# A transformer layer in float16 halves on one core: the second norm and the quantiser folded into factors, the low halves of the probabilities moved to VectorE

## The reference

```python
xn = layernorm(x, eps=1e-5)
x = x + attention(xn) + ffn(xn)

def attention(x):               # 16 heads of 16
    q = x @ Wq.T; latent = x @ Wkv_down.T           # latent has 64 columns
    k, v = latent @ Wk_up.T, latent @ Wv_up.T
    att = softmax(mask(q @ k.T / 4))  # 64 keys back, and the first 4
    return (att @ v) @ Wo.T

def bitlinear(x, w):
    xn = layer_norm(x, eps=1e-6)
    g = max(abs(xn)); x_hat = clip(xn * 128 / g, -128 + 1e-6, 128 - 1e-6) * g / 128
    w_hat = sign(round(w / (mean(abs(w)) + 1e-6))) * mean(abs(w))
    return x_hat @ w_hat.T

def ffn(x):                     # hidden width 1024
    return bitlinear(gelu(bitlinear(x, w_fc)), w_proj)
```

## Time and profile before

| what | us |
|---|---|
| median of three executions | 197.97 |
| span of the profiled execution, first to last instruction | 195.3 |
| prologue, to the first `fc` tile of batch 1 | 43.98 |
| batches 1, 2, 3, each from its first `fc` tile to the next one's | 43.02, 41.93, 35.07 |
| batch 4, from its first `fc` tile to the end of the span | 31.30 |

### The profile page before, as it was taken

The page is one execution under the profiler, slowest core; times in us unless marked ns, Lnnn a source line. Parts: engine busy times, 40 slices in busy tenths (PEclk is TensorE's granted clock), DMA queues, the critical chain, the costliest instruction groups (busy, mean ns, idle before and its releaser), DMA issues.

```text
span 195.3 us, 4915 instructions
## 1 busy us (share of the span) xinstructions
PE 160.2 (82%) x1954; PEld 106.9 (55%) x1954; DVE 148.7 (76%) x261; ACT 104.3 (53%) x152; POOL 81.9 (42%) x106
## 2 busy tenths in 40 slices
PE   1827947789978499999969499999799999997953
PEld 1515512445865466556756456647667764676731
DVE  0689999996999976655999976678997877696341
ACT  2557601356999222076997122368994314899020
POOL 6240192003089800450199601430598215059830
PEclk9999955579999755899999756999999999999975
DMA  6995000001000000013000000030000002100001
GB/s 170 334 330 168 3 2 0 3 18 38 3 3 2 0 3 0 3 54 109 0 0 0 0 0 0 0 106 5 0 0 7 0 3 65 43 3 3 0 3 54
DMA packets 7836, 7.49 MB, mean 38 GB/s; under 512 B 2500, under 2 KB 7464, under 8 KB 7720
## 3 DMA queue, kind: packets, MB, share of 16 engines
q1 hardware_dynamic: 6108, 6.02, 10.2%
q10 hardware_dynamic: 1712, 1.25, 2.1%
HBM read 6.21 MB, written 1.05 MB: 37 GB/s over the span
## 4 chain that ended last, share of the span: by engine, by line
PE 51%; DVE 26%; ACT 10%; issue 8%; DMA 2%; POOL 1%; DVEq 0%; ACTq 0%; SPq 0%
PE ring L1003 7%; PE acc L1161 7%; PE ring L1028 5%; PE ring L1122 4%; PE aux L1239 3%; PE ring L1033 3%; DVE xn L734 3%; ACT E L473 3%; PE ring L1150 3%; DVE t2s L810 3%; PE ring L1216 3%; DVE gh L803 2%; ACT EH L474 2%; PE aux L1178 2%; DVE sth L785 2%
## 5 line engine op out<-in xcount | busy, mean ns | idle before, releaser
L351 POOL TENSOR_TENSOR EL<-E,EH 128x1024 f16<-128x1024 f32 x16 | 36.3, 2296 | 37.4 <-ACT EH L474 28.4
L713 DVE TENSOR_REDUCE mx<-ring 128x4 f32<-128x768 f32 x16 | 14.7, 951 | 6.3 <-PE ring L1033 6.3
L474 ACT ACTIVATE EH<-ring,un 128x1024 f16<-128x1024 f32 x16 | 17.8, 1115 | 0.0
L473 ACT ACTIVATE E<-ring,un 128x1024 f32<-128x1024 f32 x16 | 17.8, 1112 | 0.0
L1028 PE MATMUL ring<-mask,idb 128*128 128x384 bf16 (+1 forms) x48 | 14.7, 393 | 2.2 <-DVE vs L890 2.2
L1150 PE MATMUL ring<-idf,t2s 128*128 128x128 f32 x64 | 10.4, 316 | 5.8 <-DVE Q L851 5.2
L399 POOL TENSOR_SCALAR ve<-mv 128x2 f32<-128x2 f32 x4 | 1.0, 239 | 32.5 <-DVE gx L757 32.4
L487 ACT ACTIVATE gl<-ring,a 128x1024 f32<-128x1024 f32 x8 | 8.9, 1116 | 9.1 <-PE ring L1003 9.1
L1161 PE MATMUL acc<-prT,t2h 128*128 128x256 f16 x48 | 13.2, 311 | 0.0
L1122 PE MATMUL ring<-xhT,wqT 128*128 128x256 f16 x64 | 11.1, 302 | 2.5 <-ACT EH L474 2.5
L1161 PE MATMUL acc<-prT,t2l 128*128 128x256 f16 x48 | 13.1, 309 | 0.0
(11 more groups left out here) (220 smaller groups left out, 464.7 us busy)
## 6 DMA issues: line engine op xcount, KB each, us to landing
wfc_r<-in_L_ffn_w_fc SPq DMA_DIRECT2D x1, 1024.0 KB, 7.3
wpr_r<-in_L_ffn_w_proj SPq DMA_DIRECT2D x1, 1024.0 KB, 9.6
xres<-in_L_attn_x SPq DMA_DIRECT2D x4, 256.0 KB, 2.8
out<-ob SPq DMA_DIRECT2D x4, 256.0 KB, 2.2
bias<-in_c_bias SPq DMA_DIRECT2D x1, 825.0 KB
xin<-in_L_attn_x ACTq DMA_DIRECT2D x3, 256.0 KB, 2.6
wq_r<-in_L_attn_Wq ACTq DMA_DIRECT2D x1, 256.0 KB, 3.3
xin<-in_L_attn_x SPq DMA_DIRECT2D x1, 256.0 KB, 3.9
```

The source lines that it names most:

```text
L351: nc.gpsimd.tensor_tensor(EL[at].rearrange("p g t q -> p g (t q)"), E32[:, r], EH[at].rearrange("p g t q -> p g (t q)"), ALU.subtract).the ...
L473: nc.scalar.activation(E32[:, r], src[:], ACT.Exp, scale=un[:, 0:1]).then_inc(ex[0], 1)
L474: nc.scalar.activation(EH[at].rearrange("p g t q -> p g (t q)"), src[:], ACT.Exp, scale=un[:, 0:1]).then_inc(exh[0], 1)
L713: nc.vector.tensor_reduce(out=o, in_=src[:, :, 0:2 * (T - BLK)].rearrange("p a (t k) -> p a t k", t=2), axis=AX.X, op=ALU.max).then_inc(re ...
```

## The change

- The second norm of the input rows is a factor. Since `xn` has mean zero, the feed-forward part reads `xhT` and `xlT`, and the factor `rs2`, worked out on GpSimd from the variance (`vr`, `vn`, `ve2`), goes into gelu's scale `a1`. `st2`, `mv2`, `cx`, `gx`, `txs`, their four transposes and the halves `thT`, `tlT` are gone.
- The quantiser is left out as an identity, so that `ch`, the maximum `gh`, `ghr` and `t2s` are gone. TensorE transposes `gl` itself. `gh` now names the high half of the hidden rows and `glo` the low one, both scaled by 1/gamma.
- Centring the hidden rows is done in the weights: the rows of the ternary `w_proj` get their mean subtracted once (`tsum`, `tmean`, `second_ternary`).
- The low halves of the probabilities are taken on VectorE, between other steps of the batch.
- The order is written anew: no loop, one order for all four batches. The hidden rows are transposed, and their high halves made, ahead of the exponentials; the second product stands between the rounds of scores; two rounds of the maxima come before `y` is transposed; VectorE divides after it has made `VL` and `vs`.

```diff
--- before
+++ after
 # GpSimd
-            def low_half(b, r):
...
+            def row_factors(n):
...
+                nc.gpsimd.tensor_tensor(vr[:], mv1[:, :, 1], rs1[:], ALU.mult).then_inc(row2[0], 1)
...
+                nc.gpsimd.tensor_tensor(vn[:], vr[:], rs1[:], ALU.mult).then_inc(row2[0], 1)
...
+                nc.gpsimd.tensor_scalar(ve2[:], vn[:], FFN_EPS, None, ALU.add).then_inc(row2[0], 1)
...
+                nc.gpsimd.tensor_tensor(rs2[:, n % 2, :], ve2[:], neghalf[:, 0:TT_], ALU.pow).then_inc(row2[0], 1)
 # ScalarE
+            def hidden_high(b, i):
+
+                wait(act, tr_h, b, i + 1)
...
+                nc.scalar.activation(gh[:, i].rearrange("p k n -> p (k n)"), flat(slot("t2T", b, i)),
+                                     ACT.Copy, scale=gam_r[:, 0:1]).then_inc(gh_ok[0], 1)
 # VectorE
+            def second_ternary():
+
+                dve.wait_ge(w_neg, 1)
+                for c in range(CC):
+                    did_pro(nc.vector.scalar_tensor_tensor(out=neg_t[:, 0, c * F:(c + 1) * F], in0=wpr_r[:, c, :], scalar=pthr[:, 1:2],
+                                                           in1=neg_t[:, 1, c * F:(c + 1) * F], op0=ALU.is_gt, op1=ALU.subtract,
+                                                           accum_out=tsum[:, c:c + 1]))
+                settle_pro()
+                did_pro(nc.vector.tensor_scalar(tmean[:], tsum[:], 1.0 / F, None, ALU.mult))
+                settle_pro()
+                for c in range(CC):
+                    nc.vector.tensor_scalar(tern[:, 1, c * F:(c + 1) * F], neg_t[:, 0, c * F:(c + 1) * F], tmean[:, c:c + 1], None,
+                                            ALU.subtract).then_inc(w_tern, 1)
...
+            def low_half(b, r):
+
+                gp, tp = divmod(r, 2)
+                wait(dve, ex, b, r + 1)
+                wait(dve, exh, b, r + 1)
...
+                nc.vector.tensor_tensor(EL[at].rearrange("p g t q -> p g (t q)"), E32[:, r],
+                                        EH[at].rearrange("p g t q -> p g (t q)"), ALU.subtract).then_inc(el_ok[0], 1)
 # TensorE, the batches (the whole order is new)
+                fc_tile(b, 0)
+                fc_tile(b, 1)
+                maxima_transposed(b)
+                if more:
+                    transposed_rows(b + 1)
+                sink_scores(b)
+                hidden_transposed(b, 0)
+                hidden_transposed(b, 1)
+                window_scores(b, 0)
+                window_scores(b, 1)
+                if more:
+                    latents(b + 1)
+                second_product(b, 0)
+                window_scores(b, 2)
+                second_product(b, 1)
+                window_scores(b, 3)
+                if more:
+                    q_products(b + 1)
+                    k_products(b + 1)
+                values_high(b)
+                if more:
+                    v_products(b + 1)
+                values_low(b)
+                if more:
+                    window_maxima(b + 1, 0)
+                    window_maxima(b + 1, 1)
+                attended_transposed(b)
+                if more:
+                    window_maxima(b + 1, 2)
+                output_product(b)
```

More of the change, by code:

```diff
@@ L16 @@
 VW = HD + 1
-QB = 128.0
 LN_EPS, FFN_EPS = 1e-5, 1e-6
@@ L1060, in latents, with q_products @@
+            def q_products(f):
+                if f == 0:
+                    pe.wait_ge(w_lo, 6)
+                s = take("f_q", f)
+                for t in range(NT):
                     for n, (x_half, w_half) in enumerate(HALVES):
                         for c in range(CC):
-                            last = nc.tensor.matmul(aux[:, 0:T], wkvT[:, w_half, c].rearrange("p d l -> p (d l)"), (xhT, xlT)[x_half][:, c, :],
-                                                    start=(n == 0 and c == 0), stop=(n == 2 and c == CC - 1))
@@ L1141, in hidden_transposed @@
-                def hidden_transposed(i):
-                    wait(pe, t2, b, i + 1)
-                    if front:
-                        slot("t2T", i)
-                    else:
-                        wait(pe, exh, b, 2 + i)
-                    s = hidden_slot(i, front)
-                    for k in range(FC):
-                        last = nc.tensor.transpose(s[:, k // 4, (k % 4) * P:(k % 4 + 1) * P], t2s[:, i, k * P:(k + 1) * P], idf[:])
-                    last.then_inc(tr_h[0], 1)
```

1409 lines of the change are left out of this document (632 added, 777 removed).

## The result

| | us |
|---|---|
| before, median of five executions | 198.4 (197.04 to 198.84) |
| after, median of five | 202.42 (200.75 to 205.57) |
| ratio, 95% interval | 1.0186 (1.012 to 1.0252) |
| forecast, with its range | 199.7 (194 to 205.5) |

The change makes the kernel 1.9% slower. The profiled execution took 203.39 us with a span of 201.6, so 1.8 us lie around it.

The account below looks back on a forecast made before the run. TensorE was taken as the bound, through its work, waits and clock. Prologue 46.2, three batches 111.3, last batch 31.5, clock 5.4 and way out 2.6 made a 197.0 us span; 2.7 around it gave 199.7, range 194 to 205.5.

Parts of the forecast that it names:

- Prologue: Start up to the first `fc` tile, charged with a longer second ternary step and half-clock transposes: 46.2 us (45 to 47.5).
- The step itself: Second ternary step on VectorE, ending the prologue's chain: two halves, accumulator reads, mean, subtractions; ends at 42.3 us, 1.9 later.
- The pair of subtractions: Two 1024-column mean subtractions in the second ternary step, taken at 0.7 us each; the skill's fourfold mode gave 0.8 the pair.
- The lower bound: Lower limit for one subtraction: half of VectorE's fastest pass over 1024 columns, taken as 0.35 us.
- A batch at full clock: Each of batches 1 to 3: TensorE's work 33.2 us plus waits of 1.8, 0.8, 1.1 and 0.2, making 37.1.
- the waits for `y` and `ylT`: TensorE's waits in each batch for the division, 1.8 us, and from the transposes of `y` to the output product, 0.8.
- The clock: One short fall per batch at the output product and the rounds around it: 1.8 us each, 5.4 in all.
- falls early and long: Rival: clock falls already in the row of narrow sums, keys to output product at half speed; 205.1 us, chance 0.14.
- The batch 3 that I had taken for safety: Batch 3 before the change, where products and transposes filled the place behind the sums and the clock stayed at 1.00.
- The last batch: First `fc` tile to end of `ob`: exponentials end 18.4 us in, 3.7 idle, half clock costs 1.5; 31.5 us.
- VectorE becomes the bound: Rival: low halves on VectorE cost 2.30 us as on GpSimd, 2 us more per batch; 205.7 us, chance 0.05.
- the way out: The output's way out after the last batch, 2.6 us as before.

Follow-up runs that it names:

- e2: The changed kernel with the four pieces of the narrow sums over the values spread among wide products on TensorE; 210.04 us.
- e6: e1 with an idle 240-column product after every second head of the sums over the values, 28 per batch; 216.18 us.
- e3: The changed kernel with both edits, e1's earlier division of y and e2's spread sums; 200.43 us.
- e11: e1 plus a last batch in its own order, with second product, values' products and rounds of maxima put between heads of the narrow sums; 192.76 us.
- e12: e11 with 12 idle 240-column products per batch added in the second tile's sums, 8 in the high and 4 in the low; 211.39 us.
- e1: The changed kernel with y divided on VectorE before VL and vs of the next batch are made; 198.47 us.
- e5: e1 with an idle 240-column product after every fourth head of the sums over the values, 12 per batch; 210.94 us.
- e9: e1 plus a last batch in its own order, with the low halves of the probabilities back on GpSimd; 197.48 us.

## Why the prediction was right, and where not

**The sign was right, and most of the form**: slower, inside the range; the first two batches shorter, the third and the last longer. Only the prologue went the other way, forecast 2.2 longer and measured 0.7 shorter. The forecast was 199.7, the result 202.42. That the two lie so close is in part luck: the clock cost 11.5 us more than forecast, and waits and prologue, 4.7 and 2.9 us less, hid most of it. Of its own steps, against the profiled span (197.0 forecast, 201.6 measured):

- *Prologue* (46.2; measured 43.28, 2.9 too much). The step itself was walked rightly and mis-sized in its parts, seen in VectorE's timeline:

```profile
37.76 1.27 DVE L603 SCALAR_TENSOR_TENSOR neg_t<-wpr_r,pthr,neg_t 128x1024 f16<-128x1024 f32 x1
38.96 0.07 DVE L603 DVE_READ_ACCUMULATOR neg_t<-wpr_r,pthr,neg_t 128x1 f32 x1
...
40.27 0.17 DVE L607 TENSOR_SCALAR tmean<-tsum 128x2 f32<-128x2 f32 x1
40.48 0.88 DVE L610 TENSOR_SCALAR tern<-neg_t,tmean 128x1024 f16<-128x1024 f16 x2
```

  The pair of subtractions took 0.88, not 1.4; the Trainium skill's fourfold mode ("VectorE: DVE Perf Modes", The perf-mode tier table), from which I had estimated 0.8, comes close, and the 0.7 for one that I took between the nearest rows does not. The lower bound was misread besides: VectorE's fastest pass over 1024 columns in the trace of before is that of `ch`, 942 ns, and half of it 0.47, not 0.35. The accumulator reads took 0.07 each, the second one alone behind a step, not 0.4. So the step ended at 41.4, 0.9 sooner. The transposes then ran at full clock, 1.07 for both eights instead of 1.7, and so did the last round of maxima and the first `fc` tile (3.45), for which I had charged half clock. That part is not fixed: over the profiles with this prologue the tile started between 42.9 and 45.3 and took up to 4.67.
- *A batch at full clock* (37.1, no wait for `EL`). Nothing waited for `EL`; `glo` 0.6 and `ESH` 0.7 are what was said (0.5 and 0.6). The waits for `y` and `ylT` can't be read at full clock from this kernel. Each batch waited 2.32 in all instead of 3.9. In e2, at full clock and with the sums spread, the wait for `y` was 2.7.
- *The clock* (5.4, one short fall per batch). **This is the term that was mis-sized, and its reason was wrong.** It cost 6.0, 3.3 and 7.5 us, busy time less 33.2, together 16.9; 1.5 of the 7.5 is the short trough of batch 3. 4.7 less of waits is set against that. The prediction put the fall at the end of the row, "because nothing waits from the output product on". The runs put its start inside the row of narrow sums, with TensorE busy; from there the values' products, the low sums, two rounds, the transposes and the output product all run at half. That is the rival *falls early and long*, which I gave 0.14 and priced at 205.1. Its place is the right one: the clock fell in the second tile's sums over the high halves in batches 1 and 3, and in the first tile's sums over the low halves in batch 2, at 110.9 us; that trough is the short one, some 10 us. Why the clock falls in this row the runs don't settle: e6 kept it up with denser work, and e3, e11 and e12 lost it in spite of such work. The batch 3 that I had taken for safety had the same sums, but transposes of the hidden rows on either side of the high ones, and the second product between the later steps. So those sums alone don't bring a fall either.
- *The last batch* (31.5; measured 32.3). Exponentials 18.4 us in, TensorE's wait 3.7, both as worked out; the rest ran at half clock and took 0.4 more than the 5.7 allowed, and the transposes of `y` 1.13 for 0.67.
- *The rival VectorE becomes the bound* is refuted: `EL` took 1.226 us on VectorE, and TensorE never waited for it.

In sum: prologue -2.9, batches +6.7 (forecast 116.7, measured 123.4), last +0.8, the way out as said: 4.6 of span. The 2.7 us around the span were taken from two different executions; in the profiled one they are 1.8, which takes 0.9 back.

## What to carry to other kernels

Relieving an engine pays only for the waits it causes on the bounding one: 27 us less on VectorE and 35 less on GpSimd bought 2.2 us of waits in each of two batches (the third got 0.9 more), and the order that came with it cost more. A busy TensorE is not a fast one. Read the granted clock of each stretch beside its busy time, and look for the stretch of many small products ahead of the place where it falls; a wait behind that stretch may make the trough longer. When one order is written for all batches, look at the last one by itself: with no next batch to cover it, its own chain is the bound, and reordering it gave 7.8 us between two profiles, 7.4 at the median.

## What the runs showed of the hardware that I had not expected

- TensorE's clock fell while the engine was busy without a gap, in or right beside rows of products of 17 columns (between 66 and 68 us in the changed kernel, at 72 in e1; at 107.1 in e3 among wide products behind such a row). With 28 products of 240 columns between them it stayed at 1.00 for two whole batches in e6; with 12 it held in one batch of three in e5 and in none in e12. The same instructions kept it in one batch of e11 and lost it in the next. What exactly decides it stays open.
- A change between products that use 128 columns of the array and ones that use 64 costs 0.1 us (filler 0.12 within one shape, 0.21 across; four narrow products 0.07 in a row, 0.17 between others). The values' products, which alternate between 128 and 64 rows, take 0.21 each at full clock, the queries' of the same 256 columns and always 128 rows 0.11 (2.73 for 24).
- The same kernel took from 196.5 to 206.5 us in ten executions (e1), at clocks of 0.85 to 0.78. The kernel before stayed within 196.8 to 199.7 in thirteen. More troughs alone don't make the spread: e9's profile has one of 17 us in each of batches 1 to 3, and its four executions lie within 196.6 to 198.8.
